# Twelve of sixteen group additions ahead of the second and the fourth attention: from VectorE to GpSimd

## The chip, the cores and the metric

The kernel runs on one core of one Trainium2 chip. The metric is the device time of one execution in microseconds; the time before is the median of three runs. The reader follows five engines: TensorE (PE, with its weight loads as PEld), VectorE (DVE), ScalarE (ACT), GpSimd (POOL) and SyncE (SP, which here only issues transfers). Each executes its own instructions in order and waits for the others at semaphores.

## The reference

Eight steps are applied to x, 32 sequences of 128 rows with 128 numbers each; each step adds its result to x:

```python
x = x + _L0_xattn_ref(ctx_1024, _layernorm(x), ...)
x = x + _L0_ffn_ref(_layernorm(x), ...)            # 8 experts, the best 2 of each row
x = x + _L1_xattn_ref(_layernorm(x), ctx_1024, ...)  # "second attention"
x = x + _L1_ffn_ref(_layernorm(x), ...)
x = x + _L2_xattn_ref(ctx_1024, _layernorm(x), ...)
x = x + _L2_ffn_ref(_layernorm(x), ...)            # 8 experts, the best 2 of each row
x = x + _L3_xattn_ref(_layernorm(x), ctx_1024, ...)  # "fourth attention"
x = x + _L3_ffn_ref(_layernorm(x), ...)            # 8 experts, the best 1 of each row
```

`_layernorm` subtracts from a row its mean and divides by the root of its variance. An expert stage gives two rows for each row of x, already weighted; what matters here is the addition x = x + y0 + y1, and the mean and variance that the attention behind it takes of the sum.

## The kernel before

x stays in SBUF as the tile X (`x_rows`), 128 partitions by 32 sequences by 128 numbers. The 32 sequences are handled as eight groups of four (G = 4, NG = 8); a group of X is 128x512. An attention runs in two turns of four groups (TURNS = 2, W = 4): groups 0 to 3 in turn 0, groups 4 to 7 in turn 1. Within a turn the four groups are four streams, woven together step by step on each engine (`weave`).

An expert stage leaves its rows in DRAM. When the second or the fourth attention begins (`attention_1(0)` and `attention_3(2)` in the code), SyncE fetches them group by group with `load_pairs` (L1709), 512 KB each, into YY, which lies in `paired_rows`; the four groups of turn 1 are each issued once the group four before them has landed. A semaphore for each stream, `pairs_here`, tells of the landing.

VectorE adds them in `combine` (L566): for each group two additions of 128x512, each followed by a drain (`ch.link`), so that the second sees what the first wrote. `combine_stream` waits for the landing and calls `combine`. `next_rows` calls `combine_stream` and then `known`: four `bn_stats` (L480) and four `bn_aggr` (L476) of the group, which give mean and variance. The four groups of turn 0 are done in a row before anything else; those of turn 1 are put between the steps of turn 0 (rounds (1, 1, 1, 0, 1) in the second attention, (2, 2) in the fourth).

Then `head_norms` turns the variances into scales: one instruction on VectorE (L456), two on ScalarE (`roots_by_log`), three on VectorE (L449 to L451), and sixteen `tensor_scalar` of 128x128 (L498), four for each stream, which write the normed rows `u_rows`. After each four TensorE may start on that stream (L665). The attention follows: in the second, q on TensorE (L1859), L1778 and L1779 on VectorE, exp on ScalarE, L1878 on TensorE, L1791 to L1798 on VectorE, the projection (L1859 again) and its addition to x (L1801). In the fourth: scores (L2638), maxima (L2746), exp (L2684), the mixing (L2646) and L2755 on VectorE, which divides and adds x.

GpSimd has nothing to do in the second attention. In the fourth it fills `last_pad` (L2604 and L2606) and much later scatters rows (L2614). `Chain.link` is a drain of the engine's pipeline.

Of the kernel before, what the change touches and what calls it, by code (L numbers as in the profile page):

```python
# [13 lines left out]
ALU = mybir.AluOpType  # L14
# [11 lines left out]
G = 4  # L26
NG = B // G
# [92 lines left out]
def build(nc, A, out):  # L120
    with ExitStack() as top:
# [11 lines left out]
        def counter(name):  # L133
            return Counter(top.enter_context(nc.semaphore(name)))
# [5 lines left out]
        X = sb("x_rows", [P, B, P])  # L140
# [5 lines left out]
        YY = PAIRED[:, 0:2 * B * P].rearrange("p (t k d) -> p t k d", k=2, d=P)  # L146
# [52 lines left out]
        W = 4  # L199
# [25 lines left out]
        pairs_here = [counter(f"pairs_here{w}") for w in range(W)]  # L225
# [16 lines left out]
        probs_scaled = counter("probs_scaled")  # L242
        pairs_staged = counter("pairs_staged")
        pairs_combined = counter("pairs_combined")
        latents_normed = counter("latents_normed")
        context_normed = counter("context_normed")
        latents_turned = counter("latents_turned")
# [49 lines left out]
        def group(t, g):  # L297
            return t[:, bass.ds(g * G, G), :]
# [17 lines left out]
        with ExitStack() as ph:  # L316
            block = ph.enter_context(nc.Block(no_gpsimd_drain=True))
# [219 lines left out]
        def next_rows(dve, ch, i, st, here, rounds):  # L537

            if i < TURNS:
# [6 lines left out]
                    yield  # L546
                assert w == W

        def combine_stream(dve, ch, i, w, layer):

            dve.wait_ge(pairs_here[w].sem, i * 16 + (pairs_here[w].value + 16))
            combine(dve, ch, i * W + w, layer)

        def close_streams(SS, ctx=False):
            for c in (spread_known, roots_made):
# [6 lines left out]
        def combine(dve, ch, g, layer):  # L562

            own = group(X, g)
            for k in range(CHOICES[layer]):
                ch.link(dve.tensor_tensor(own, own, YY[:, bass.ds(g * G, G), k, :], ALU.add))  # L566
# [641 lines left out]
        CHOICES = {0: 2, 1: 2, 2: 2, 3: 1}  # L1208
# [502 lines left out]
        def close_rows(layer):  # L1711
            for c in pairs_here:
                c.value += 16 * TURNS

        def load_expert_weights(sp, layer):

# [16 lines left out]
        def attention_1(layer_before):  # L1733
            assert layer_before in SCATTERED
            with ExitStack() as ph:
# [16 lines left out]
                @block.sync  # L1752
                def _(sp):
                    load_pairs(sp, layer_before)
                    sp.dma_start(ctx_turned_dram, flat(CTT[:, :, :])).then_inc(ctx_put_away.sem, 16)
                    sp.wait_ge(SS[W - 1].dve.sem, SS[W - 1].DVE.at(TURNS - 1, "u_normed"))
                    sp.dma_start(head_raw[:, 0:INNER], A["L2_xattn_Wq"]).then_inc(weights_x.sem, 16)
                    sp.dma_start(head_raw[:, INNER:3 * INNER], A["L2_xattn_Wkv"]).then_inc(weights_x.sem, 16)
                    sp.dma_start(head_o.rearrange("p (c d) -> p c d", d=P), A["L2_xattn_Wo"].rearrange("(c p) d -> p c d", p=P)).then_inc(weights_x.sem, 16)
                    for S in SS:  # L1760
                        sp.wait_ge(S.pe.sem, S.PE.at(TURNS - 1, "out"))
                    load_expert_weights(sp, 1)
                    sp.wait_ge(ctx_put_away.sem, 16)

                @block.vector
                def _(dve):
# [792 lines left out]
        def attention_3(layer_before):  # L2559
            SCALE = float(P) ** -0.5  # L2560
            with ExitStack() as ph:
# [26 lines left out]
                @block.sync  # L2588
                def _(sp):
                    sp.dma_start(mask[:, :], mask_dram[1:2, :]).then_inc(masks_loaded.sem, 16)  # L2590
                    load_pairs(sp, layer_before)
                    load_expert_weights(sp, 3)
                    sp.wait_ge(last_pad_made.sem, 1)
                    for n in range(SPARE_TILES):
                        sp.dma_start(xlast[E * REGION + n * P:E * REGION + (n + 1) * P, :], last_pad[:, :]).then_inc(spare_tiles_stored.sem, 16)
                    place_last_pads(sp, last_pad, range(E // 2))
                    sp.wait_ge(pads_placed.sem, 2 * 16 * E)
                    sp.wait_ge(spare_tiles_stored.sem, 16 * SPARE_TILES)
                    sp.wait_ge(rows_spread.sem, 16 * (2 * B + B))
                    load_first_tiles(sp, 3)  # L2600

                @block.gpsimd
                def _(pool):
                    pool.memset(last_pad[:, :], 0.0)  # L2604
                    pool.drain()
                    pool.tensor_copy(last_pad.bitcast(U32)[:, LAST_TO:LAST_TO + 1], spare_row[:, 0:1]).then_inc(last_pad_made.sem, 1)  # L2606
                    for i in range(TURNS):
                        for w in range(W):
                            pool.wait_ge(SS[w].act.sem, SS[w].ACT.at(i, "tail_kept"))
                            pool.wait_ge(positions_made.sem, NG + i * W + w + 1)  # L2610
                            if i < TURNS - 1:
                                pool.wait_ge(SS[W - 1].act.sem, SS[W - 1].ACT.at(i + 1, ("u_turned", "q_kept", "exp", "p_turned")[w]))
                            for t in range(w * G, (w + 1) * G):
                                pool.indirect_dma_start(xlast, bass.IndirectOffsetOnAxis(ap=spots[:, i, t:t + 1], axis=0), LAST_ROWS[:, i * N + t, :], None).then_inc(rows_spread.sem, 16)  # L2614
# [253 lines left out]
```

## Time and profile before

| what | value |
|---|---|
| median of three runs | 1673.55 us |
| the three runs | 1673.93, 1673.55, 1666.23 us |
| profiled execution, its own time | 1664.46 us |
| profiled execution, span | 1662.6 us |
| granted TensorE clock, mean of the span | 0.897 |
| busy: PE, DVE, ACT, POOL | 1398.9, 1121.4, 903.6, 767.3 us |

The span runs from the first instruction of the profiled execution to the last. The second attention lies between about 355 and 488 us of it, the fourth between about 1438 and 1562 us. In a row of the timeline stand the start, the duration, the engine, the line of the kernel, the operation, what it writes and reads, how many such instructions are merged into the row, and in brackets how long the engine sat idle before it and what ended that.

### The profile page before, as it was taken

What the parts mean: (1) busy time and instruction counts of PE and PEld (TensorE: products, weight loads), DVE (VectorE), ACT (ScalarE), POOL (GpSimd) and SP (SyncE); (2) the same over time, 40 slices, a digit from 0 to 9 for tenths busy, and PEclk for the clock granted to TensorE, in tenths of its full rate; (3) what the DMA queues carried; (4) which work ended last, traced back from release to release, by engine and by line L of the source; (5) the groups of instructions that cost most, each with busy time, mean ns of one, the idle gap of its engine ahead of it and who ended that gap; (6) DMA issues with size and microseconds to landing.
All of it is one profiled execution on the core that took longest, in us unless ns stands there. A gap on an engine that the chain in (4) does not pass through costs nothing. (4 is left out here: it accounts for less than half of the span.)

```text
span 1662.6 us, 37562 instructions
## 1 busy us (share of the span) xinstructions
PE 1398.9 (84%) x10866; PEld 1301.8 (78%) x10867; DVE 1121.4 (67%) x3528; ACT 903.6 (54%) x2726; POOL 767.3 (46%) x775
## 2 busy tenths in 40 slices
PE   6687699946877389999999999999998399667398
PEld 4566599945666289999999999999998399545298
DVE  5646755558767367778787877878776466576455
ACT  4354155522323178777778787777775134244254
POOL 4066444420004454556757575757554456303344
PEclk9797899977657699999999999999999699878599
DMA  9201122250220300000000000000000323531322
GB/s 233 34 32 57 52 57 67 64 182 1 103 75 30 123 14 1 14 2 19 10 16 10 7 19 0 25 0 13 1 14 6 107 79 84 164 103 52 115 81 70
DMA packets 88412, 88.70 MB, mean 53 GB/s; under 512 B 17058, under 2 KB 74761, under 8 KB 87927
## 3 DMA queue, kind: packets, MB, share of 16 engines
q1 hardware_dynamic: 72472, 58.20, 12.8%
q0 software_dynamic: 12448, 26.27, 4.6%
q10 hardware_dynamic: 3392, 3.02, 0.7%
q8 instruction: 47, 0.77, 0.2%
q14 instruction: 53, 0.43, 0.1%
HBM read 54.06 MB, written 34.91 MB: 54 GB/s over the span
## 5 line engine op out<-in xcount | busy, mean ns | idle before, releaser
L2130 POOL TENSOR_TENSOR paired_rows<-paired_rows,rinv 128x1024 f32<-128x1024 f32 x128 | 242.7, 1896 | 243.6 <-DVE rinv L2451 228.6
L2442 DVE TENSOR_TENSOR probs_turned_lo<-psum_banks,probs_turned_hi 128x512 fp32r<-128x512 f32 x256 | 175.5, 686 | 137.7 <-ACT probs_turned_hi L2295 133.3
L2321 ACT ACTIVATE paired_rows<-psum_banks,neg_max 128x256 f32<-128x256 f32 x512 | 237.2, 485 | 0.6 <-DVEq L2022 0.4
L2242 PE MATMUL psum_banks<-probs_turned_hi,y_rows 128*128 128x256 f32 x1024 | 214.8, 293 | 0.9 <-DVEq L2022 0.9
L2192 PE MATMUL psum_banks<-y_turned_parts,queries_hi 128*128 128x256 f32 x1024 | 199.6, 293 | 3.0 <-DVEq L2022 3.0
L2242 PEld LDWEIGHTS psum_banks<-probs_turned_hi,y_rows 128*128 128x128 f32 x1024 | 167.5, 190 | 1.7 <-DVEq L2022 1.6
L2295 ACT CAST probs_turned_hi<-psum_banks 128x512 fp32r<-128x512 f32 x256 | 151.2, 591 | 19.9 <-PE psum_banks L2163 8.3
L2192 PEld LDWEIGHTS psum_banks<-y_turned_parts,queries_hi 128*128 128x128 f32 x1024 | 157.7, 190 | 3.6 <-issue 3.6
L2163 PE MATMUL psum_banks<-ident,paired_rows 128*128 128x128 f32 x1024 | 155.5, 274 | 5.3 <-DVE probs_turned_lo L2442 2.9
L2457 DVE TENSOR_REDUCE neg_max<-psum_banks 128x4 f32<-128x1024 f32 x128 | 155.4, 1214 | 3.7 <-PE psum_banks L2192 3.5
L2192 PE MATMUL psum_banks<-y_turned_parts,queries_lo 128*128 128x256 f32 x512 | 145.0, 283 | 0.0
L2242 PE MATMUL psum_banks<-probs_turned_lo,y_rows 128*128 128x256 f32 x512 | 144.5, 282 | 0.0
L2295 ACT CAST queries_hi<-psum_banks 128x512 fp32r<-128x512 f32 x128 | 75.0, 586 | 106.0 <-PE psum_banks L2228 97.6
L2163 PEld LDWEIGHTS psum_banks<-ident,paired_rows 128*128 128x128 f32 x1024 | 116.7, 140 | 8.7 <-DVE probs_turned_lo L2442 3.6
L1601 ACT ACTIVATE hidden<-psum_banks,tile_w 128x128 f32<-128x128 f32 x284 | 81.4, 368 | 65.4 <-PE psum_banks L1564 51.2
L1539 POOL DMA_INDIRECT expert_rows<-expert_rows_sb,tile_rows x71 | 68.1, 959 | 97.1 <-DVE expert_rows_sb L1648 94.8
L2321 ACT ACTIVATION_READ_ACCUMULATOR paired_rows<-psum_banks,neg_max 128x1 f32 x512 | 110.2, 215 | 0.0
L2228 PE MATMUL psum_banks<-y_turned_parts,wqk_hi 128*128 128x256 f32 x512 | 103.8, 295 | 0.8 <-POOL y_turned_parts L2054 0.8
L2242 PEld LDWEIGHTS psum_banks<-probs_turned_lo,y_rows 128*128 128x128 f32 x512 | 97.7, 191 | 0.0
L2192 PEld LDWEIGHTS psum_banks<-y_turned_parts,queries_lo 128*128 128x128 f32 x512 | 97.1, 190 | 0.0
L745 POOL DMA_INDIRECT rows_by_expert_first<-paired_rows,top_experts x64 | 62.5, 976 | 70.7 <-DVE mix_weights L1126 49.3
L1539 POOL DMA_INDIRECT expert_rows<-expert_rows_sb__,tile_rows x71 | 68.2, 960 | 58.1 <-ACT expert_rows_sb__ L1608 57.4
(721 smaller groups left out, 3787.1 us busy)
## 6 DMA issues: line engine op xcount, KB each, us to landing
paired_rows<-expert_rows SPq DMA_DIRECT2D x16, 512.0 KB, 6.0
expert_w_a<-rows_by_expert_last SPq DMA_DIRECT2D x39, 129.0 KB
tile_rows<-rows_by_expert_first SPq DMA_DIRECT2D x71, 65.0 KB
tile_rows<-rows_by_expert SPq DMA_DIRECT2D x71, 65.0 KB
expert_w_b<-in_L_ffn_w_dram SPq DMA_DIRECT2D x2, 2048.0 KB, 12.6
tile_rows<-expert_rows SPq DMA_DIRECT2D x8, 512.0 KB, 3.7
x_rows<-in_x_dram SPq DMA_DIRECT2D x8, 256.0 KB, 5.4
ctx_turned_dram<-ctx_turned SPq DMA_DIRECT2D x1, 2048.0 KB, 11.1
```

Source lines behind the costliest of these rows:

```text
L745: pool.indirect_dma_start(xfirst, bass.IndirectOffsetOnAxis(ap=first_spots[:, i, k, t:t + 1], axis=0), ROWS[:, i * N + t, :], None).then_i ...
L1539: pool.indirect_dma_start(ys, bass.IndirectOffsetOnAxis(ap=to, axis=0), yo[:, i % SLOTS, :], None).then_inc(expert_out[i % SLOTS].sem, 16)
L1601: ins = act.activation(hidT[:, s % 2, c * P:(c + 1) * P], hidden_bank(s, c // 2)[:, c % 2 * P:(c % 2 + 1) * P], ACT.Gelu, bias=w1[:, s % 4 ...
L2130: ins = pool.tensor_tensor(probs[:, k, :, :], probs[:, k, :, :], rinv[:, k, :].unsqueeze(2).to_broadcast([P, 4, 256]), ALU.mult)
L2163: ins = pe.transpose(bank[T_BANK][:, h * P:(h + 1) * P], probs[:, par, h, c * P:(c + 1) * P], ident[:, :])
L2192: ins = pe.matmul(bank[S_BANKS[par] + r][:, h * 256:(h + 1) * 256], queries[q][:, h, r, :], yparts[:, 2 * s2 + y, r * 256:(r + 1) * 256], ...
L2228: ins = pe.matmul(bank[Q_BANK][:, h * 256:(h + 1) * 256].rearrange("p (r q) -> p r q", r=2), wqk_parts[w][:, 2 * u3 + h, :], latents_of, s ...
L2242: ins = pe.matmul(bank[Z_BANK][:, r * 256:(r + 1) * 256], yrows[:, 2 * s1 + y, (2 * r + k) * P:(2 * r + k + 1) * P], probsT[x][:, (u + 1) ...
L2295: ins = act.copy(dst, bank[bank_][:, :])
L2321: ins = act.activation(probs[:, par, h, :], bank[S_BANKS[par] + h // 2][:, (h % 2) * 256:(h % 2 + 1) * 256], ACT.Exp, bias=nmax[:, par, h: ...
L2442: ins = dve.tensor_tensor(lo, bank[bank_][:, :], hi.bitcast(F32), ALU.subtract)
L2457: ins = dve.tensor_reduce(nmax[:, par, :], ps[:, S_BANKS[par]:S_BANKS[par] + 2, :].rearrange("p r (h k) -> p (r h) k", k=256), AX.X, ALU.m ...
```

## The change

`POOL_GROUPS` holds the groups 2 to 7. Their additions are made by GpSimd, in the order of the groups, each with the wait for the landing that VectorE had; the second addition of a group raises the new semaphore `pairs_added`. VectorE keeps groups 0 and 1 whole. For the other six it waits for `pairs_added` and takes the statistics as before. In the fourth attention GpSimd does this after `last_pad`, before its scatters.

```diff
+        pairs_added = counter("pairs_added")
...
+        POOL_GROUPS = [g for g in range(NG) if g >= W // 2]
+
         def combine_stream(dve, ch, i, w, layer):
 
+            g = i * W + w
+            if g in POOL_GROUPS:
+                dve.wait_ge(pairs_added.sem, pairs_added.value + POOL_GROUPS.index(g) + 1)
+                return
             dve.wait_ge(pairs_here[w].sem, i * 16 + (pairs_here[w].value + 16))
-            combine(dve, ch, i * W + w, layer)
+            combine(dve, ch, g, layer)
+
+        def combine_on_pool(pool, layer):
+
+            for g in POOL_GROUPS:
+                i, w = g // W, g % W
+                pool.wait_ge(pairs_here[w].sem, i * 16 + (pairs_here[w].value + 16))
+                for k in range(CHOICES[layer]):
+                    if k:
+                        pool.drain()
+                    ins = pool.tensor_tensor(group(X, g), group(X, g), YY[:, bass.ds(g * G, G), k, :], ALU.add)
+                ins.then_inc(pairs_added.sem, 1)
...
         def close_rows(layer):
             for c in pairs_here:
                 c.value += 16 * TURNS
+            pairs_added.value += len(POOL_GROUPS)
...
+                @block.gpsimd
+                def _(pool):
+                    combine_on_pool(pool, layer_before)
...
                     pool.tensor_copy(last_pad.bitcast(U32)[:, LAST_TO:LAST_TO + 1], spare_row[:, 0:1]).then_inc(last_pad_made.sem, 1)
+                    combine_on_pool(pool, layer_before)
                     for i in range(TURNS):
```

Both layers concerned have CHOICES = 2, so GpSimd makes twelve additions in each of the two attentions and VectorE keeps four in each.

## Rows read from the trace of the kernel before

**Rows 1.** The page's first part: busy time, share and instructions of each engine.

```profile
PE 1398.9 (84%) x10866; PEld 1301.8 (78%) x10867; DVE 1121.4 (67%) x3528; ACT 903.6 (54%) x2726; POOL 767.3 (46%) x775
```

**Rows 2.** The timeline at the start of the second attention.

```profile
355.46 8.78 SPq L1709 DMA_DIRECT2D paired_rows<-expert_rows  x8
359.37 1.46 DVE L566 TENSOR_TENSOR x_rows<-x_rows,paired_rows 128x512 f32<-128x512 f32 x2 [6.99 <-DMA paired_rows<-expert_rows]
...
370.47 0.38 DVE L476 BATCH_NORM_AGGREGATE mean_var__<-norm_stats__ 128x2 f32<-128x6 f32 x4
...
371.71 0.17 DVE L449 TENSOR_TENSOR newton__<-rstd__ 128x16 f32<-128x16 f32 x1 [0.57 <-ACT rstd__ L465]
...
373.64 1.12 PE L665 MATMUL psum_banks<-ident,u_rows 128*128 128x128 f32 x4 [22.03 <-DVE u_rows L498]
...
375.56 1.11 DVE L498 TENSOR_SCALAR u_rows___<-x_rows,mean_var__,rstd__ 128x128 f32<-128x128 f32 x4
```

**Rows 3.** By source line: the additions L566 (ns min/median/max) and the landing of L1709.

```profile
L566 DVE TENSOR_TENSOR x_rows<-x_rows,paired_rows x32: 656/691/693, 359.4 to 1475.8; 128x512 f32<-128x512 f32 x32
...
DMA to landing us min/median/max: 3.9/6.0/7.1
```

**Rows 4.** By source line: GpSimd's addition of two full tiles, in the third attention.

```profile
L2071 POOL TENSOR_TENSOR x_rows<-x_rows,paired_rows x14: 1285/1292/1303, 602.1 to 1126.1; 128x512 f32 x10, 128x512 f32<-128x512 f32 x4
```

**Rows 5.** Timelines of DVE and POOL at 572 and 723 us; L2365 by source.

```profile
572.33 0.41 DVE L449 TENSOR_TENSOR rows_work<-rows_rstd 128x8 f32<-128x8 f32 x1 [6.35 <-ACT rows_rstd L2281]
...
573.07 0.55 DVE L451 SCALAR_TENSOR_TENSOR rows_rstd<-rows_work,rows_rstd 128x8 f32<-128x8 f32 x1
...
572.33 0.40 POOL L2052 COPY y_turned_copy<-expert_w_b 128x256 f32<-128x256 f32 x1
572.88 0.72 POOL L2054 TENSOR_TENSOR y_turned_parts<-expert_w_b,y_turned_parts 128x256 fp32r<-128x256 f32 x1
...
723.13 0.77 POOL L2054 TENSOR_TENSOR y_turned_parts<-expert_w_b,y_turned_parts 128x256 fp32r<-128x256 f32 x1
...
L2365 DVE COPY scale_of_rows<-rows_rstd x2: 158/432/706, 723.1 to 723.2; 128x4 f32<-128x4 f32 x2
```

**Rows 6.** Small POOL copies beside the norms L498, in the first attention.

```profile
135.04 0.32 POOL L750 COPY paired_rows<-mix_weights 128x4 f32<-128x4 f32 x1 [5.32 <-ACT u_turned L642]
...
L750 POOL COPY paired_rows<-mix_weights x8: 198/204/322, 119.0 to 183.0; 128x4 f32<-128x4 f32 x8
...
L498 DVE TENSOR_SCALAR u_rows___<-x_rows,mean_var_,rstd_ x8: 339/341/343, 64.8 to 135.9; 128x128 f32<-128x128 f32 x8
```

**Rows 7.** Second attention, DVE behind the places of groups 5 and 6, both turns.

```profile
387.71 0.72 DVE L1791 RECIPROCAL d_inv<-psum_banks 128x96 f32<-128x96 f32 x1
...
403.81 0.69 DVE L1801 TENSOR_TENSOR x_rows<-x_rows,psum_banks 128x512 f32<-128x512 f32 x1 [0.98 <-PE psum_banks L1859]
...
446.43 0.76 DVE L1791 RECIPROCAL d_inv<-psum_banks 128x96 f32<-128x96 f32 x1 [2.58 <-PE psum_banks L1878]
...
462.56 0.69 DVE L1801 TENSOR_TENSOR x_rows<-x_rows,psum_banks 128x512 f32<-128x512 f32 x1 [3.75 <-PE psum_banks L1859]
```

**Rows 8.** The timeline of the fourth attention: its head, its two turns.

```profile
1442.89 1.46 DVE L566 TENSOR_TENSOR x_rows<-x_rows,paired_rows 128x512 f32<-128x512 f32 x2 [3.88 <-DMA paired_rows<-expert_rows]
...
1446.01 0.36 POOL L2606 CAST last_pad<-spare_row 128x1 uint32<-128x1 f32 x1 [7.26 <-issue]
...
1454.00 0.38 DVE L476 BATCH_NORM_AGGREGATE mean_var____<-norm_stats____ 128x2 f32<-128x6 f32 x4
...
1468.79 0.69 DVE L2746 TENSOR_REDUCE neg_max<-psum_banks 128x4 f32<-128x512 f32 x1 [3.14 <-PE psum_banks L2638]
...
1476.02 3.82 PE L2646 MATMUL psum_banks<-ctx_rows,expert_w_a 128*128 128x128 f32 x32
...
1479.14 1.13 DVE L2755 SCALAR_TENSOR_TENSOR paired_rows<-psum_banks,rinv,x_rows 128x128 f32<-128x128 f32 x4
...
1510.35 0.99 POOL L2614 DMA_INDIRECT rows_by_expert_last<-paired_rows,top_experts  x1 [63.98 <-ACT u_turned___ L2677]
...
1522.66 3.82 PE L2646 MATMUL psum_banks<-ctx_rows,expert_w_a 128*128 128x128 f32 x32
...
1523.84 1.13 DVE L2755 SCALAR_TENSOR_TENSOR paired_rows<-psum_banks,rinv,x_rows 128x128 f32<-128x128 f32 x4 [1.52 <-PE psum_banks L2646]
```

## The prediction

> **What bounds the kernel now.** I read the page first: TensorE is busy for 84% of the span, VectorE for 67%, GpSimd for 46% [rows 1]. These are means over stages with different limits, and the change touches two short ones, so I went to the timelines of the second and the fourth attention.
>
> At the start of the second attention everything waits for VectorE [rows 2]. The transfers are issued from 355.46 us, group 0 is there at 359.37, and until 370.85 (370.47 + 0.38) VectorE adds four groups and takes their statistics: 11.48 us, 2.75 for each after the first. TensorE has been idle for 22.03 us when L665 starts at 373.64, released by the first four of the sixteen norms L498; the last of these end at 376.67. One addition takes 0.69 us [rows 3], the two of a group with their drains some 1.53, which leaves 1.25 for the statistics. In the fourth attention the same head runs from 1442.89 to 1454.38 [rows 8].
>
> The groups of turn 1 are another matter. The place behind group 5 in turn 0 (L1791 at 387.71, without a wait) has the same work in front of it in turn 1, with no additions, and there VectorE idles 2.58 us; the place behind group 6 shows 0.98 us of waiting for TensorE with additions and statistics in front and 3.75 us without [rows 7]. The difference, 2.77, is the whole of group 6's work. So these lie in waits for TensorE and are free now.
>
> **The change, part by part.** The sum is made against the profiled execution's own 1664.46 us (span 1662.6), which is 0.5% under the median of the three runs, 1673.55; the differences are put on the median. About 0.5%, 8.4 us, is what a measurement of this kernel can tell from no change.
>
> Removed: twelve additions on VectorE in each attention. Added: as many on GpSimd. One with two full tiles takes 1.29 us there [rows 4]; between a copy that ends at 572.73 and the next instruction behind a drain lie 0.15 us [rows 5]. A pair is thus about 2.7 us, and twelve about 16.3. Landings: group 0 after 3.9 us, the median 6.0, the longest 7.1 [rows 3]. With about 1.5 us between groups, group 2 is there at 362.3. GpSimd's additions alone would run from 362.3 to 378.6, over the same time in which VectorE adds group 1, scales, and writes the sixteen norms (until 376.67). So the question is what the two engines do to each other.
>
> The trace answers it for three kinds of instruction [rows 5]. L449 reads two tiles in SBUF; 0.17 is its usual length [rows 2], but at 572.33 it takes 0.41 and ends at 572.74, as GpSimd's copy does (572.73). L451 takes 0.55 and ends at 573.62; GpSimd's instruction ends at 573.60. Of two copies on VectorE (L2365, from 723.1 to 723.2), the first takes 0.158 and the second 0.706, to the end of a GpSimd instruction that began at 723.13 and ends at 723.90. So VectorE waits out a whole GpSimd instruction, and GpSimd gets in between two VectorE instructions that stand in a row. For the norms L498 there is one trace: GpSimd's copy L750 takes 0.20 as a rule and 0.32 at 135.04, where L498 runs in a row (the last at 135.9) [rows 6]. L498 holds what GpSimd needs; whether L498 itself would stand still for 1.29 us no row shows, because it never meets a long GpSimd instruction. Its bounds are 0 and 1.29 us for each addition that it meets. I take 1.29, as the three kinds in rows 5 did.
>
> The Trainium skill, page "SBUF — State Buffer", section "Who interferes with whom", says that GpSimd and VectorE share one pair of SBUF ports, that the one that starts first has it for its whole instruction, and that `tensor_scalar`, like a copy, can take the pair. By it L498 would wait like the copy and the sum would be the one below; without it, the third case below. Rows 5 agree for the copy and the two-input instructions.
>
> *Second attention, head.* Groups 0 and 1 cost VectorE 2.75 each as before, plus one wait: its second addition of group 1 meets GpSimd's first of group 2 (+1.25). GpSimd's second waits 0.65 for VectorE's, so group 2 is summed at about 365.9 and group 3, whose additions meet only statistics (one input, and I take no wait for them), at about 368.6. Four statistics of group 3 end at 369.9: 0.95 sooner than 370.85. Then come one L456, L449 to L451 and sixteen L498. At that moment GpSimd has six to seven of its additions left (groups 5 to 7). In turn, one addition, one VectorE instruction: the next six or so of VectorE each wait about 1.29, together 7.7. Net: 7.7 − 0.95 = +6.8, with GpSimd done at about 380 and the last norm at 383.4 in place of 376.67. The first stream is as late: its fourth norm ends at about 380.3. Nothing absorbs this, for TensorE and ScalarE wait for these rows [rows 2].
>
> *Second attention, turn 1's groups.* All summed by 380, and their additions were free: 0. What covers the statistics that stay is the same wait for TensorE.
>
> *Fourth attention, head.* GpSimd must first finish `last_pad`; L2606 stood still for 7.26 us for no releaser in the profile and ended at 1446.37, when group 2 has just landed (1445.8). By the same steps group 3's statistics end at 1453.6 in place of 1454.38, then six additions of 1.29 get in the way: 7.7 − 0.8 = +7.0.
>
> *Fourth attention, turn 0.* Groups 4 and 5 end in a wait of 3.14 us for TensorE [rows 8]: 0. Groups 6 and 7 do not: L2755 starts 3.12 us after L2646 (1476.02 to 1479.14) but 1.18 us after it in turn 1 (1522.66 to 1523.84), where no group stands in front. Without 4 x 0.76 = 3.06 us of additions, L2755 starts when the mixing allows: 3.12 − 1.18 = −1.94, and behind it VectorE works without a stop.
>
> Queues: SyncE issues and waits as before. GpSimd's scatters L2614 start at 1510.35 [rows 8], 46 us after its last addition would end (about 1464), so nothing is late there. The new waits on VectorE stand in front of statistics; queued behind the two in a head are the scales and norms for which TensorE and ScalarE wait.
>
> **Sum:** 6.8 + 7.0 − 1.9 = +11.9 us, 1676.4 for the profiled execution and 1685 on the median.
>
> **The rivals.**
>
> *No meeting (other side).* L498 and L449 to L451 do not lose to GpSimd, because VectorE's instructions follow each other too closely. Then the head ends when group 3 is summed and its statistics are done: 368.9 in place of 370.85, norms 2.1 sooner; 1.5 in the fourth, where GpSimd starts at 1446.4; 1.9 in turn 0. Together −5.5: 1668. It decides if the sixteen norms keep 0.26 us from start to start. For it: in rows 6 L498 kept its 0.34 us while GpSimd's copies lost. Against: that copy has 4 numbers, not 512, and rows 5.
>
> *Only two-input instructions wait.* L498 goes free, L449 to L451 and the addition of group 1 do not. Three instructions lose about 1.25 each less the gain of the head: +1.8 and +2.1, with −1.9: +2.0, 1675.5.
>
> *GpSimd starts late.* L2606 stood still for 7.26 us behind the start of its block [rows 8]. If GpSimd's first wait-and-add in the second attention stands as long or 2 us longer, the first addition comes at 362.8 to 364.7: nothing more, or +1.4, and a stall between additions would hold VectorE directly, since group 3's statistics wait for GpSimd. A 3 us stall in each attention gives about +2 more each: +16, 1689.5.
>
> **How the numbers follow.** The waits in turn: 0.60. GpSimd late on top: 0.10. Only two-input instructions: 0.16. No meeting: 0.14. The predicted time is that of the first, 1685. The range goes from 1670, between the second and the no-meeting case, to 1692, the late case with the scatter of the three runs (7.7 us apart); it leaves out most of the no-meeting case and a little above. Slower by over 8.4 us: nearly all of the first and the late case, less what scatter takes back, 0.62. Within: 0.34. Faster by over 8.4: no case reaches it, only −5.5 with scatter, 0.04.
>
> **What would show it.** In the changed kernel's profile: 8 additions L566 on VectorE and 24 of about 1.3 us on GpSimd; in the second attention some of L449 to L451 and the first L498 at 1.0 to 1.5 us, each ending with a GpSimd addition; TensorE's first L665 near 380 in place of 373.64; L2755 1.2 us behind L2646 in turn 0 of the fourth. The forecast is wrong if L498 keeps 0.34 us beside additions of 1.29, if GpSimd is done long before VectorE scales, or if turn 1's statistics wait for `pairs_added`.

## The result and the profile after

The changed kernel takes 1684.74 us (median of six runs, 1675.18 to 1689.6) where the kernel before, on the same chip, takes 1670.77 (six runs, 1666.23 to 1674.72): ratio 1.0085, interval 1.0059 to 1.0112. It is slower, by some 14 us or 0.85%. The profiled execution took 1675.65 us (span 1673.9, mean granted clock 0.899), 11.2 more than that of before (1664.46); it was one of the two quick ones of the six. The sum in the prediction was +11.9 and its time 1685. The total fits; the parts it is made of do not, as the traces show.

The page's first part and its row of the granted clock, for the changed kernel:

```profile
PE 1396.2 (83%) x10866; PEld 1298.9 (78%) x10867; DVE 1118.2 (67%) x3504; ACT 902.3 (54%) x2726; POOL 796.3 (48%) x799
...
PEclk9797899977667799999999999999999699778599
```

Against [rows 1], GpSimd is busy for 29 us more, the 24 additions. VectorE is busy for only 3.2 us less, though it lost 24 additions of 0.69 us (16.6 us): what it saved it spends in instructions that stand still. The head of the second attention shows them. Below is its timeline in the changed kernel (start, duration, engine, line, operation, count, idle time before and its end). All lines of the code have moved by 1 to 24: L566 is L584, L498 is L499, L449 to L451 are L450 to L452, L665 is L683.

```profile
357.20 1.46 DVE L584 TENSOR_TENSOR x_rows<-x_rows,paired_rows 128x512 f32<-128x512 f32 x2 [7.13 <-DMA paired_rows<-expert_rows]
...
359.98 2.33 DVE L584 TENSOR_TENSOR x_rows<-x_rows,paired_rows 128x512 f32<-128x512 f32 x2
360.26 1.50 POOL L569 TENSOR_TENSOR x_rows<-x_rows,paired_rows 128x512 f32<-128x512 f32 x1 [8.96 <-DMA paired_rows<-expert_rows]
...
368.71 14.49 POOL L569 TENSOR_TENSOR x_rows<-x_rows,paired_rows 128x512 f32<-128x512 f32 x11 [6.96 <-issue]
370.01 0.87 DVE L481 BATCH_NORM_STATS2 norm_stats__<-x_rows 128x6 f32<-128x128 f32 x4 [6.31 <-POOL x_rows L569]
...
372.63 0.87 DVE L481 BATCH_NORM_STATS2 norm_stats__<-x_rows 128x6 f32<-128x128 f32 x4 [1.30 <-POOL x_rows L569]
...
374.36 0.89 DVE L457 TENSOR_SCALAR newton__<-mean_var__ 128x16 f32<-128x16 f32 x1
...
376.80 1.08 DVE L452 SCALAR_TENSOR_TENSOR rstd__<-newton__,rstd__ 128x16 f32<-128x16 f32 x1
377.95 3.87 DVE L499 TENSOR_SCALAR u_rows<-x_rows,mean_var__,rstd__ 128x128 f32<-128x128 f32 x4
381.75 2.06 DVE L499 TENSOR_SCALAR u_rows_<-x_rows,mean_var__,rstd__ 128x128 f32<-128x128 f32 x4
...
381.88 1.11 PE L683 MATMUL psum_banks<-ident,u_rows 128*128 128x128 f32 x4 [32.57 <-DVE u_rows L499]
...
384.75 1.10 DVE L499 TENSOR_SCALAR u_rows___<-x_rows,mean_var__,rstd__ 128x128 f32<-128x128 f32 x4
```

Two things are to be seen. First, from the end of group 3's statistics (374.24) to the last norm (385.85) it takes 11.6 us, where before [rows 2] it was 5.8: the small scales, L451 apart, and the first four norms stand at three to six times their length while GpSimd adds. That was forecast. Second, GpSimd makes its first addition at 360.26, when the rows are there, and then stands for 6.96 us with no releaser. VectorE waits 6.31 us for group 2 because of it, and the statistics end 17.0 us after the first addition, not 11.5. The forecast had a stall between additions in its late case alone, at 0.10. From first addition to last norm the head takes 28.65 us in place of 17.30: +11.35. By source line, the stall is in the drain ahead of the second addition (ns, minimum, median and maximum):

```profile
L568 POOLq DRAIN  x12: 1500/2522/8401, 360.2 to 1462.7; - x12
```

The third attention, which the change does not touch, begins sooner behind the second. First the kernel before, then the changed one, GpSimd's timeline:

```profile
558.27 0.19 POOL L2058 COPY group_scale<-ctx_rstd 128x4 f32<-128x4 f32 x1 [1.78 <-POOLq L1446]
567.71 1.04 POOL L2060 TENSOR_TENSOR context_normed<-ctx_rows,ctx_mean_var 128x512 f32<-128x512 f32 x1 [9.25 <-issue]
```

```profile
568.81 0.18 POOL L2081 COPY group_scale<-ctx_rstd 128x4 f32<-128x4 f32 x1 [1.79 <-POOLq L1464]
571.78 1.04 POOL L2083 TENSOR_TENSOR context_normed<-ctx_rows,ctx_mean_var 128x512 f32<-128x512 f32 x1 [2.78 <-issue]
```

A drain lies between the two instructions. It cost 9.25 us before and costs 2.78 now, and TensorE waits for its result there. The fourth attention, changed kernel, timeline:

```profile
1446.80 1.46 DVE L584 TENSOR_TENSOR x_rows<-x_rows,paired_rows 128x512 f32<-128x512 f32 x2 [3.77 <-DMA paired_rows<-expert_rows]
...
1450.02 0.26 POOL L2629 CAST last_pad<-spare_row 128x1 uint32<-128x1 f32 x1 [7.26 <-issue]
1450.24 1.25 POOL L569 TENSOR_TENSOR x_rows<-x_rows,paired_rows 128x512 f32<-128x512 f32 x1
...
1461.15 3.87 DVE L499 TENSOR_SCALAR u_rows<-x_rows,mean_var____,rstd____ 128x128 f32<-128x128 f32 x4
...
1485.73 1.13 DVE L2779 SCALAR_TENSOR_TENSOR paired_rows<-psum_banks,rinv,x_rows 128x128 f32<-128x128 f32 x4 [1.51 <-PE psum_banks L2670]
...
1504.70 0.19 DVE L516 COPY logits<-psum_banks 128x32 f32<-128x32 f32 x1 [1.51 <-PE psum_banks L649]
...
1508.11 0.19 DVE L516 COPY logits<-psum_banks 128x32 f32<-128x32 f32 x1 [1.51 <-PE psum_banks L649]
```

Here the drain's 7.26 us lie ahead of the additions, inside the filling of `last_pad`, as in [rows 8]. The head takes 22.25 us where it took 17.26 (+5.0). From the last norm to L2779 (L2755 before) it is 16.7 us where it was 19.0 (-2.3). From there to the last copy of the logits it is 22.6 where it was 19.4 (+3.2): the four copies come 1.71 us apart and not 0.89 to 1.20, since the matmuls ahead of them run at the lower clock (0.50 granted from 1500 to 1512 us).

So that the experiments can be compared, each execution is cut at the same landmarks: (A) start to first addition of the second attention, code that nobody changed; (B) from there to the last norm of the head; (C) to the end of the last addition to x (L1801 before) of its turn 1; (D) to TensorE's first transpose in the third attention; (E) to the first addition of the fourth; (F) to its last norm; (G) to the last logits copy; (H) to the last scatter of the output. Times in us, one profiled execution each, worked out from the timelines:

| kernel | A | B | C | D | E | F+G | H |
|---|---|---|---|---|---|---|---|
| before | 359.4 | 17.3 | 92.8 | 100.5 | 872.9 | 55.7 | 162.4 |
| changed | 357.2 | 28.65 | 93.0 | 95.3 | 872.6 | 61.5 | 163.7 |
| e1 | 361.6 | 28.65 | 96.8 | 93.8 | 875.4 | 54.9 | 163.3 |
| e2 | 364.9 | 17.3 | 92.5 | 101.7 | 871.1 | 61.4 | 163.1 |
| e3 | 360.2 | 22.4 | 97.5 | 102.9 | 875.6 | 62.3 | 161.8 |
| e4 | 358.9 | 17.3 | 101.3 | 92.5 | 873.9 | 53.4 | 163.9 |
| e5 | 364.9 | 24.95 | 96.8 | 95.3 | 874.9 | 61.6 | 165.5 |
| e6 | 367.3 | 22.1 | 97.6 | 95.9 | 878.8 | 62.3 | 162.2 |
| e7 | 359.8 | 17.3 | 92.6 | 94.8 | 876.5 | 58.2 | 165.7 |
| e8 | 361.1 | 17.3 | 92.6 | 95.4 | 877.9 | 59.4 | 162.7 |
| e9 | 359.5 | 22.3 | 92.3 | 95.3 | 871.6 | 62.0 | 162.0 |
| e10 | 364.9 | 17.3 | 92.7 | 95.7 | 875.7 | 58.1 | 165.5 |
| e11 | 361.4 | 17.3 | 92.6 | 94.8 | 875.7 | 55.5 | 162.9 |
| e12 | 360.4 | 17.3 | 92.6 | 95.5 | 873.0 | 55.3 | 164.1 |

B repeats to 0.02 us between kernels that do the same there; A, E and H have nearly the same code in all and yet scatter by 10, 8 and 4 us. So a mechanism is read from B to D, F and G, and a whole from the runs.

### The profile page after: what moved, and what is told of

It reads as the page before. It is cut to its first block and busy times, and to the rows that moved or that the text cites. A ratio compares the mean times of both kernels' runs of the same rounds, so it can differ in the third digit from the quotient of the medians.

```text
span 1673.9 us, 37550 instructions
## 1 busy us (share of the span) xinstructions
PE 1396.2 (83%) x10866; PEld 1298.9 (78%) x10867; DVE 1118.2 (67%) x3504; ACT 902.3 (54%) x2726; POOL 796.3 (48%) x799
## 6 DMA issues: line engine op xcount, KB each, us to landing
ctx_turned_dram<-ctx_turned SPq DMA_DIRECT2D x1, 2048.0 KB, 10.4
```

## The experiments

**e1 and e2: one attention at a time.** In e1 the fourth attention adds on VectorE as before, in e2 the second.

```diff
-            if g in POOL_GROUPS:
+            if g in POOL_GROUPS and layer == 0:      # e2: layer == 2
...
-            pairs_added.value += len(POOL_GROUPS)
+            pairs_added.value += len(POOL_GROUPS) if layer == 0 else 0
...
-                    combine_on_pool(pool, layer_before)      # in the attention that adds on VectorE
```

> Only the second attention's additions are on GpSimd; the fourth attention adds on VectorE as before. Theory A (as predicted: additions and norms take turns, about 1 us of waiting each, and nothing else happens): the second head's norms end 7 us later than before, measured from the first addition. Theory B (the traces compared so far: besides the turns, worth 5.8 us, GpSimd stands still for 7 us behind its first addition, worth 6.5 us, and the third attention starts 5 us sooner behind its own first drain): first addition to last norm 28.6 us instead of 17.3 (+11.3), third attention's TensorE idle time 10.5 instead of 17, whole kernel +5.5 us (0.3%) by the landmarks. In the fourth attention both expect the numbers of before: statistics end 11.5 us and norms 17.3 us after the first addition, the head and turn 0 together +0.

> Only the fourth attention's additions are on GpSimd; the second attention adds on VectorE as before. Theory A: the fourth head +7, turn 0 -1.9, whole kernel +5 us. Theory B: head +5 (statistics 1.1 sooner, turns 6.1), L2755's place 2.3 us regained, and 3 us lost because TensorE is granted less in turn 0 after it idled longer: whole kernel +5.5 to +6 us. The third attention should start as before: GpSimd 9.25 us behind the start of its block, TensorE idle 17 us. If it starts 5 us sooner here too, then its sooner start has nothing to do with GpSimd's block in the second attention, and theory B's -5 is wrong.

e1: 1680.8 us, ratio 1.0069 (1.0044 to 1.0094). e2: 1672.34, ratio 1.0021 (1.0006 to 1.0037). The two add up to 1.0090, and the whole change has 1.0085: nothing passes between the parts that the times could show. The second attention carries three quarters of the loss. In e1 the head takes 28.65 us as in the changed kernel and GpSimd's stall is 6.95 us; D is 93.8. In e2 the head of the second attention is 17.3 and the third attention stalls for the full time, so the sooner start goes with GpSimd's block in the second attention:

```profile
574.16 1.04 POOL L2079 TENSOR_TENSOR context_normed<-ctx_rows,ctx_mean_var 128x512 f32<-128x512 f32 x1 [9.26 <-issue]
```

e1 is 6 us slower than theory B's +5.5. Some 4 of them are C, 96.8 in place of 92.8; e9 returns to that. F in e1 is 17.1 us, as before.

**e3: no drain between the two additions.**

```diff
                 for k in range(CHOICES[layer]):
                     if k:
-                        pool.drain()
+                        ins.then_inc(half_added.sem, 1)
+                        pool.wait_ge(half_added.sem, half_added.value + POOL_GROUPS.index(g) + 1)
```

> As the changed kernel, but between the two additions of a group GpSimd waits on a semaphore that the first sets, instead of draining. H1, the stall belongs to the first drain of a block: the 7 us behind the first addition are gone, statistics of group 3 end about 10.5 us after the first addition, norms about 17 + 6 = 23 us instead of 28.6, whole kernel 4 to 6 us faster than the changed one (if the third attention's first drain then stalls for its full 9.25 us again, those 5 us are lost again and the whole kernel is the same). H2, GpSimd gets its instructions late whatever they are: the stall stays at 6 to 8 us, at the second addition or close to it, and the whole kernel is the same as the changed one.

1685.11 us, ratio 1.009 (1.0067 to 1.0113). GpSimd's timeline in e3, second attention and start of the third:

```profile
363.28 15.98 POOL L571 TENSOR_TENSOR x_rows<-x_rows,paired_rows 128x512 f32<-128x512 f32 x12 [8.82 <-DMA paired_rows<-expert_rows]
...
571.27 0.18 POOL L2084 COPY group_scale<-ctx_rstd 128x4 f32<-128x4 f32 x1 [1.78 <-POOLq L1466]
580.71 1.04 POOL L2086 TENSOR_TENSOR context_normed<-ctx_rows,ctx_mean_var 128x512 f32<-128x512 f32 x1 [9.25 <-issue]
```

All twelve additions are in one row without a gap, and the head takes 22.4 us. The stall belongs to the drain (H1). And as H1's bracket said, the third attention's drain is then the first one again, at 9.25 us: what e3 gained in the head it paid 200 us later. H2 falls.

**e4: GpSimd takes the groups of turn 1 alone, behind the head.**

```diff
-        POOL_GROUPS = [g for g in range(NG) if g >= W // 2]
+        POOL_GROUPS = [g for g in range(NG) if g >= W]
...
+            pool.wait_ge(S.dve.sem, S.DVE.at(0, "u_normed"))      # S: stream 3 of the attention
             for g in POOL_GROUPS:
```

> GpSimd adds only groups 4 to 7, and only after the last norm of stream 3 of turn 0, so that no addition meets the head's scales and norms and no statistics in the head wait for GpSimd. If the loss comes from the head alone (meeting and late groups), both heads are those of before: 17.3 us from first addition to last norm. L2779's place in turn 0 of the fourth attention comes 1.5 to 2 us sooner; the whole kernel is 2 us faster than before if the third attention's start is as before, 7 us faster if GpSimd's block in the second attention takes 5 us off the third attention's start. Theory A (no such stall) gives -2. Against: VectorE's work between the norms and the scores may meet GpSimd's additions instead (up to 8 x 1.29 = 10 us if each is waited for in turn).

1670.08 us, ratio 1.0015 (0.9997 to 1.0033): no gain, a miss. Both heads are those of before, as expected. But the stall has come along, and now it stands ahead of what VectorE needs in turn 0. GpSimd and VectorE in e4's timeline:

```profile
376.26 1.27 POOL L570 TENSOR_TENSOR x_rows<-x_rows,paired_rows 128x512 f32<-128x512 f32 x1 [23.07 <-DVE u_rows___ L499]
384.49 9.17 POOL L570 TENSOR_TENSOR x_rows<-x_rows,paired_rows 128x512 f32<-128x512 f32 x7 [6.96 <-issue]
...
385.78 0.87 DVE L481 BATCH_NORM_STATS2 norm_stats__<-x_rows 128x6 f32<-128x128 f32 x4 [9.60 <-POOL x_rows L570]
```

C grows by 8.5 us and D shrinks by 8.0. The drain here comes 24 us after the last scatter was issued and still costs 6.96 us, to the hundredth what it costs 10 us after it in the changed kernel: time that passes does not shorten it. Whether it depends on how many scatters there were is another question; the last section has the rows for it. In the fourth attention F+G is 53.4 in place of 55.7, the 2.3 us of turn 0.

**e5: the groups of turn 1, at once.** As e4, without its wait.

> GpSimd adds only groups 4 to 7 (turn 1's) in both attentions, and as soon as their rows are there; VectorE adds groups 0 to 3, so no statistics in the head wait for GpSimd. If additions and norms take turns: in the second attention the statistics of group 3 still end some 11.5 us (up to 14, where additions meet) after the first addition, GpSimd's first addition lies near 365 us, its drain stands for 7 us, and the other seven additions fall on the norms: 6 to 7 of them at 1.0 us of waiting each, so first addition to last norm 23 to 24.5 us in place of 17.3. Without such turns it is 17.3. In the fourth attention, where the drain's 7.26 us lie ahead of the additions, eight additions meet additions and statistics of groups 2 and 3 instead: +3 to +7.

1680.99 us, ratio 1.007 (1.0043 to 1.0097). This is the meeting of additions and norms alone. VectorE and GpSimd in e5's timeline:

```profile
370.43 2.36 DVE L584 TENSOR_TENSOR x_rows<-x_rows,paired_rows 128x512 f32<-128x512 f32 x2
...
378.94 3.08 DVE L499 TENSOR_SCALAR u_rows<-x_rows,mean_var__,rstd__ 128x128 f32<-128x128 f32 x4
379.19 9.30 POOL L569 TENSOR_TENSOR x_rows<-x_rows,paired_rows 128x512 f32<-128x512 f32 x7 [6.96 <-issue]
381.93 3.96 DVE L499 TENSOR_SCALAR u_rows_<-x_rows,mean_var__,rstd__ 128x128 f32<-128x128 f32 x4
385.82 3.02 DVE L499 TENSOR_SCALAR u_rows__<-x_rows,mean_var__,rstd__ 128x128 f32<-128x128 f32 x4
388.76 1.10 DVE L499 TENSOR_SCALAR u_rows___<-x_rows,mean_var__,rstd__ 128x128 f32<-128x128 f32 x4
```

No statistics wait for GpSimd here; one addition meets the two of group 2 (2.36 for 1.43), and seven additions meet the twelve norms of streams 0 to 2, which take 10.0 us for 3.3. The fourth four, behind GpSimd's last addition (388.49), take 1.10 again. The head takes 24.95 us: 0.9 for the statistics and 6.7 for the norms, 0.96 us for each of the seven additions. In the fourth attention the head is 21.9, +4.6, inside the range given. The no-meeting rival and the rival in which only two-input instructions wait are excluded: L499 reads one tile of data.

**e6: one drain more, ahead of everything.**

```diff
                 @block.gpsimd
                 def _(pool):
+                    pool.drain()
                     combine_on_pool(pool, layer_before)
```

> As the changed kernel, with one drain more on GpSimd as the first instruction of the second attention's block, where GpSimd waits for rows anyway. If the 7 us belong to the first drain after the scatters, whenever it comes (e3 and e4 point to this): the stall lies ahead of the first addition, no L569 has more than 0.2 us of issue in front of it, the second head measures 22.5 us from first addition to last norm as without drains (e3: 22.4) instead of 28.6, the third attention's first drained instruction still waits 2.8 us and not 9.25, and the whole kernel is 6 us faster than the changed one, 1678 on the scale where that is 1684. If the stall needs an addition in front of it, it stays where it was, and nothing changes.

1684.63 us, ratio 1.0079 (1.0053 to 1.0106). The profile does what was expected: the twelve additions stand in one row (370.35, 16.40 us), B is 22.1 and the third attention's drain costs 2.78. The whole does not, a miss: the 6 us less in the head cannot be seen in the time. In this profile C is 97.6, as in e1, e3 and e5 (96.8 to 97.5), and A, which e6 does not touch, is 8 us longer than before.

**e7: the kernel before, with one drain.**

```diff
+                @block.gpsimd
+                def _(pool):
+                    pool.drain()
+
```

> The kernel before with one drain on GpSimd in the second attention, where it has nothing to do, and nothing else. If the first drain costs some 7 us once and the next one within the following stages does not: the third attention's wait in front of its first drained instruction falls from 9.25 to 2.8 us, TensorE's idle time there from 16.95 to 10.5, and the whole kernel is 6.5 us faster than before (ratio 0.996). If the change in the third attention came from the additions, or from there being a block of GpSimd's with more instructions, it stays at 9.25 and the time is that of before.

1665.42 us, ratio 0.998 (0.9959 to 1.0001). By source line, the drain in the second attention, and GpSimd in the third:

```profile
L1767 POOLq DRAIN  x1: 6846/6846/6846, 355.6 to 355.6; - x1
```

```profile
562.07 1.04 POOL L2064 TENSOR_TENSOR context_normed<-ctx_rows,ctx_mean_var 128x512 f32<-128x512 f32 x1 [2.78 <-issue]
```

A single drain, at a time when GpSimd has no other work, takes 6.85 us, and the one that TensorE waits for 200 us later falls from 9.25 to 2.78. D is 94.8. The whole is 3.3 us faster by the ratio; the interval just holds the expected 6.5, and just holds no change too.

**e8: e7's drain, and e4's additions in the fourth attention alone.**

> The kernel before with one drain on GpSimd in the second attention, all additions there on VectorE, and in the fourth attention GpSimd adding groups 4 to 7 after the last norm of turn 0. Third attention -6.5 if e7's theory holds; fourth attention, by e4's profile (first addition to the last copy of the logits 2.3 us shorter) -2.3: together -8.8 us, ratio 0.9947. If the drain does nothing: -2, ratio 0.9988.

1669.3 us, ratio 0.9998 (0.9978 to 1.0017): a miss. D is 95.4, so the drain works. In the fourth attention L2755's place comes 19.1 us behind the last norm, no sooner than before, and then it is another 23.1 to the last logits copy, where before had 19.4: TensorE was granted 0.84 from 1460 to 1480 us and e4, which gained there, 0.93. The 2.3 us are smaller than what moves in the same place without any change: L2755 comes 18.3 us behind the last norm in e1, 18.4 in e7 and 19.0 before, all three with the same code there. That it is the clock is argued, not shown.

**e9: TensorE kept at work in the second attention's head.** As e6, and TensorE transposes the identity while it waits. The bank is written again before anyone reads it.

```diff
+        def keep_busy(pe, bank_, n):
+            for _ in range(n):
+                turn_group(pe, bank_, lambda j: ident[:, :])
...
+                    keep_busy(pe, T[W - 1]["B"], 48)
                     for i in range(TURNS):
                         weave(body(w, i, SS[w], T[w]) for w in range(W))
```

> As e6 (the changed kernel with one drain ahead), and TensorE does 48 groups of four transposes of the identity into a bank that it writes later anyway (0.54 us a group at the full clock), while it waits for the rows of the second attention's head. Theory clock: where TensorE has idled 27 to 33 us in this head, it is granted 0.50 to 0.52 in the 15 us behind (e1, e3), and the stretch from the last norm to the last L1801's place takes 96.8 to 97.6 us, against 92.5 to 92.8 where it idled 22 us (before, e2, e7, e8). With TensorE kept at work the stretch takes 90 to 93 us with 0.9 or more granted in the first 15 us, and the whole kernel is 5 us faster than e6, ratio to before near 1.005. If the 4 us come from something else (the order in which additions and norms leave the streams), the stretch stays at 97.

1669.7 us, ratio 0.9984 (0.9961 to 1.0007), where e6 has 1.0079. The stretches of TensorE in e6 and then in e9, before, in and behind the 15 us from its first transpose of the rows (busy time and count, granted clock, DMA share, GB/s):

```profile
340.00:385.40 45.40, 19.23 (x168) 0.74 0.50 167
385.40:400.40 15.00, 14.11 (x52) 0.50 0.00 0
```

```profile
340.00:378.90 38.90, 34.92 (x291) 0.91 0.53 181
378.90:393.90 15.00, 13.33 (x94) 1.00 0.01 1
```

In e6 TensorE idled for 26.1 us and then worked at 0.50, the lower of its two levels (1.2 GHz); in e9 it worked through and had 1.00. B is the same (22.1 and 22.3), so the norms' time has nothing to do with it, but C falls from 97.6 to 92.3: 5.3 us. So the head's lateness costs twice, once itself and once because TensorE, idle for longer, comes back at the lower level. The ratios differ by 0.95% or 16 us (10 to 22 with both intervals), more than these 5.3 and more than the 5 us expected; the rest of it is not explained.

**e10, e11 and e12: the same for a faster kernel.** e10 is e7 with 36 such groups in the second attention; e11 has 10 and 16 more in the fourth, ahead of and behind its first matmuls; e12 is e11 with e8's additions on GpSimd.

```diff
+                    keep_busy(pe, T[W - 1]["B"], 10)
...
+                        if w == 0 and not i:
+                            keep_busy(pe, T[W - 1]["B"], 16)
```

> As e7 (the kernel before with one drain in the second attention), and TensorE does 36 groups of four transposes of the identity (19.4 us) while it waits in the head of the second attention. First addition to last norm stays at 17.3. If the granted clock behind the head sets part of the time: from 0.86 and 0.66 in the two stretches behind the first transpose up towards 1.0, last norm to last L1801 2 to 3 us shorter than the 92.6 of e7, whole kernel 2 to 3 us faster than e7, ratio to before 0.994 to 0.996. If VectorE and ScalarE set that stretch, nothing changes against e7 (0.996 to 0.998).

> As e10, and in the head of the fourth attention as well: 10 groups ahead of its first matmuls and 16 behind them (14 us together). Theory clock: from the last norm there to the last copy of the logits it took 38.4 us before, 40.9 in e7 and 42.2 in e8 with the same code there or less work, so that this stretch swings with the clock; kept busy it takes 36 to 38, and the whole kernel is 2 to 4 us faster than e10, ratio 0.992 to 0.994. If it does not: same as e10.

> As e11, and in the fourth attention GpSimd adds groups 4 to 7 after the last norm of turn 0, as in e8. By e4's profile this takes 2.3 us off the stretch from the first addition to the last copy of the logits: ratio to before 0.9945 where e11 has 0.9959, 1.5 to 2.5 us faster than e11. If VectorE waits in turn 0 of the fourth attention for GpSimd's additions (e8 was not faster than e7: 1669.3 against 1665.4), it is the same as e11 or up to 3 us slower, and the term of -1.9 us for turn 0 of the fourth attention is worth nothing in the whole.

e10: 1665.66 us, ratio 0.9961 (0.9942 to 0.998). e11: 1664.96, ratio 0.9959 (0.9934 to 0.9984). e12: 1663.74, ratio 0.9958 (0.9942 to 0.9973). All three beat both kernels, the one before by some 7 us. That is about what the drain takes off D; but e7, with the drain alone, came to 3.3, and the intervals don't tell the four from one another, so what each part adds is not shown. Keeping TensorE busy where it idles 22 us gained nothing in C (92.7 against 92.6 in e7), and what was expected of it in the fourth attention did not come either: F+G is 55.5 in e11, less than e10's 58.1, but no less than the 55.7 of before, and the whole is that of e10. The turn-0 gain of GpSimd's additions is in e12's trace (L2755's place 15.5 us behind the last norm, 18.8 in e11) and is lost again at the logits, which come 1.71 us apart there and 0.89 in e11. First e12, then e11, VectorE's timeline:

```profile
1490.44 0.19 DVE L516 COPY logits<-psum_banks 128x32 f32<-128x32 f32 x1 [1.52 <-PE psum_banks L650]
1492.14 0.19 DVE L516 COPY logits<-psum_banks 128x32 f32<-128x32 f32 x1 [1.51 <-PE psum_banks L650]
```

```profile
1494.82 0.19 DVE L515 COPY logits<-psum_banks 128x32 f32<-128x32 f32 x1 [0.70 <-PE psum_banks L631]
1495.72 0.19 DVE L515 COPY logits<-psum_banks 128x32 f32<-128x32 f32 x1 [0.70 <-PE psum_banks L631]
```

## Why the prediction was right, and where its steps were not

The time was right; of its three terms one was right and two were sized wrongly, and three effects that the sum did not have came on top and cancelled in part. That the total fits to a few us is in part luck.

*The waits in turn.* Right as a mechanism, shown by e5 with nothing else in play. The Trainium skill, page "SBUF — State Buffer", section "Who interferes with whom", has the one that starts first keep the pair of ports for its whole instruction; by that rule a `tensor_scalar` like L499 waits like the copy of [rows 5], and e5's norms of up to 1.3 us agree. The size was too large: the prediction took 1.29 us for each of six. In e5 it is 0.96 each. In the changed kernel seven of VectorE's instructions behind the statistics wait 5.8 us together, 0.83 each, because part of each addition runs while VectorE is between instructions or waits for ScalarE. The statistics never wait (0.87 beside GpSimd's additions as before), as the prediction took. Its +6.8 for the second head is +5.1 where no stall disturbs it (e3, 22.4; 4.8 in e6), its +7.0 for the fourth is +5.0 in the changed kernel and in e2. The gain ahead of it was sized well: group 3's statistics end 10.4 us after the first addition in e3, 1.06 sooner than before, where 0.95 was said.

*GpSimd's stall.* The step that failed was the choice that GpSimd starts adding at once in the second attention. The prediction had seen the 7.26 us ahead of L2606, taken them for a late start of the block and given it 0.10, with most of it hidden behind the landing of the rows; it named a stall between additions there, but at 3 us and some +2 in each attention. It is the first drain, and it lies between the first and the second addition, the worst place: +6.2 us in B (28.65 against 22.4 without drains, 22.1 with the drain ahead). This was worth as much as the meeting.

*The third attention.* No step and no rival had it: what the drain in the second attention takes, the first drain of the third no longer does, and the kernel before had it all there, in front of TensorE. With a drain in the second attention, D is 93.8 to 95.9 in ten kernels and 92.5 in e4, and 100.5 to 102.9 in the three that have no drain there: -6.5 us (95.2 against 101.7 in the mean, e4 left out). It gives back the whole stall.

*Turn 1's groups.* Right: they were put at nothing, and C is 93.0 in the changed kernel as in the one before (92.8). The cover has an end: in e4, where the stall makes them late, VectorE waits 9.60 us for them and C is 8.5 longer.

*Turn 0 of the fourth attention.* Right: -1.94 was said, -2.3 came in the changed kernel and in e4. It is not seen in any whole, because the stretch behind it swings by more: +3.2 in the changed kernel.

*The clock.* The prediction has no term for it. TensorE idles 10 us longer in the second head, and the profiles with such a head have C at 96.8 to 97.6 in four of five; the changed kernel's own profiled execution is the fifth, at 93.0, with 0.75 granted in the first 15 us, not 0.50. That is part of why its difference, 11.2, lies under the median's 14; A, 2.2 us shorter with the same code, is another. Without the clock the terms are 5.1 + 6.2 - 6.5 + 5.0 - 2.3 = +7.5; the 4 of C and the 3.2 of the logits would make it 14.7. That this meets the median's 14 is not shown to be more than chance: the 3.2 come in e7 and e10 too, whose fourth attention is that of before (22.5 us from L2755 to the last logits, 19.4 before), so they may not belong to the change at all, and A, E and H scatter by more than what is left.

Of the prediction's own tests, the 8 additions on VectorE and the 24 on GpSimd, L499 at up to 1.3 us, TensorE's first L683 near 380 (381.88) and L2779 earlier in turn 0 all hold. None of them would have told the stall from the waits. "Faster" was rightly near zero, and the no-change case of 0.34 was not far: the lower end of the interval is 0.59% slower.

## What to carry to other kernels

Work moved to an engine that is off the critical path must be placed by what the busy engine does in the same microseconds: an addition of 1.26 us on GpSimd beside VectorE's copies and scales costs VectorE 0.8 to 1 us each, and costs nothing beside its statistics. An idle time that the profile puts down to nothing ("issue") at the head of a block is a cost with an owner: find the instruction and let the engine pay it where nobody waits. Here one drain ahead took 6.5 us off the third attention, and e7, e10, e11 and e12, which have it, came out 0.2 to 0.4% under the kernel before; e8, which has it too, did not. A stretch in which TensorE waits longer can cost again behind it, through the granted clock; where the gain sought is below 3 us, that decides more than the change.

## What the runs showed of the hardware

The first drain on GpSimd in the second attention takes 6.85 us with nothing before it in its block (e7) and holds the next addition for 6.95 or 6.96 us in four kernels (changed, e1, e4, e5), whether that addition would be due 10 or 24 us after the last scatter. The first of the third attention costs 2.78 us where there was one in the second, and 9.25 where there was none; in the fourth it costs 7.25 or 7.26 in every kernel looked at.

What sets the size can be read from the traces: the number of indirect transfers (gathers and scatters, `DMA_INDIRECT`) that GpSimd issued since its last drain. By source line, the transfers of the kernel before between 200 and 560 us, and the drains of the line whose first stands at the start of the third attention, before and in e7:

```profile
L1539 POOL DMA_INDIRECT expert_rows<-expert_rows_sb,tile_rows x71: 957/960/969, 213.9 to 352.7; - x71
...
L1539 POOL DMA_INDIRECT expert_rows<-expert_rows_sb_,pair_rows x16: 956/977/1374, 523.9 to 555.5; - x16
...
L1530 POOL DMA_INDIRECT tile_rows<-normed_rows_dram,source_rows x16: 943/968/1535, 514.7 to 546.7; - x16
...
L2059 POOLq DRAIN  x8: 2002/2004/9346, 558.3 to 1138.4; - x8
...
L2063 POOLq DRAIN  x8: 1999/2001/2874, 559.1 to 1135.8; - x8
```

A drain's record begins before the instruction ahead of it is done; counted from that instruction's end, the drains of the kernel before take at most 0.08 us with no transfer since the last drain (110 of them, from 60 us on), 0.31 behind three, 0.47 behind five (0.8 where the last of the five was issued 2.6 us earlier), and 7.17 behind the 87 ahead of the fourth attention. Behind the 32 ahead of the third it is 2.68 in e7. That is some 0.08 us for each, so the wait is not paid once and for all: each drain seems to pay for the transfers since the one before. Behind 135 (64 of the first attention and the 71 above) it is 6.85, behind all 167 it is 9.15, less for each; if the 64 are left out, 0.09 to 0.10. Why these count for less, and what the engine does in that time, no run shows, and none was made to vary the number of transfers by itself.

The Trainium skill, page "GPSIMD Engine Reference", section "2.1 Instruction dispatch", names one cost of this kind: the first call of a freshly loaded GpSimd kernel pays for the loading of its code, about 6 us, with no instruction in the profile. The size is near, and the idle time without a releaser fits; but a single loading would not be 0.31 us behind three transfers, 2.68 behind 32 and 7.17 behind 87, so the rows speak against it.

TensorE's clock behind a wait: after 22 us of idling the next 15 us had 0.84 to 0.87 (before, e2, e4, e7, e8), after 25 to 33 us 0.50 to 0.52 in e1, e3, e5 and e6 and 0.75 in the changed kernel, and kept busy 1.00 (e9 to e12). The scatter of the runs goes with it: over the 100 runs of the kernel before that stand beside the experiments, the time and the mean granted clock are correlated with -0.84, and code that no kernel changed (A) took 357 to 367 us.
